# Rows turned by DMA instead of TensorE, and expert weights in a ring of three slots, in a mixture-of-experts stage on one core

## What is computed

```
logits = einsum('bld,ed->ble', layernorm(h) * rn_g + rn_b, router_w) + router_b
top_w, top_idx = top_k(logits, 2);  top_w = softmax(top_w)
for e in range(8):
    t = layernorm(h) * ln_g[e] + ln_b[e]
    t = gelu(t @ w1[e] + b1[e])          # 256 -> 1024, exact gelu
    t = t @ w2[e] + b2[e]                # 1024 -> 256
    out += combine[..., e] * t
x = x + gb * out
```

## Time and profile before

| | |
|---|---|
| three runs | 1261.82 us median, 1258.67 to 1263.27 |
| profiled execution | 1263.39 us |
| its span, first to last instruction | 1261.6 us |
| mean granted TensorE clock over the span | 0.909 |
| PE, DVE, ACT, POOL busy | 1123.1, 912.2, 554.1, 588.1 us |

### The profile page before, as it was taken

The page is one execution under the profiler, slowest core; times in us unless marked ns, Lnnn a source line. Parts: engine busy times, 40 slices in busy tenths (PEclk is TensorE's granted clock), DMA queues, the critical chain, the costliest instruction groups (busy, mean ns, idle before and its releaser), DMA issues.

```text
span 1261.6 us, 29766 instructions
## 1 busy us (share of the span) xinstructions
PE 1123.1 (89%) x8408; PEld 892.3 (71%) x8408; DVE 912.2 (72%) x2923; ACT 554.1 (44%) x1098; POOL 588.1 (47%) x487
## 2 busy tenths in 40 slices
PE   5789799889884329999999999999999999999996
PEld 1334454554443318998999999998999999998995
DVE  5577878877886426777777777777777777777775
ACT  1567565666563203433444444433434444433442
POOL 2111554554556572455554454445554444445553
PEclk8788878877796558999999999999999999999998
DMA  5346546556454265877444747457444444445743
GB/s 159 126 155 210 175 154 230 194 179 229 153 179 141 75 217 166 213 208 179 87 84 85 215 90 213 85 128 176 88 84 86 85 85 82 85 87 116 192 83 45
DMA packets 105765, 177.38 MB, mean 141 GB/s; under 512 B 23580, under 2 KB 76968, under 8 KB 99592
## 3 DMA queue, kind: packets, MB, share of 16 engines
q1 hardware_dynamic: 71560, 120.34, 30.7%
q0 software_dynamic: 34176, 56.72, 23.2%
HBM read 228.66 MB, written 63.69 MB: 232 GB/s over the span
## 4 chain that ended last, share of the span: by engine, by line
PE 71%; DVE 9%; issue 4%; POOL 3%; DMA 2%; another core or an unknown queue 1%; ACT 1%; DVEq 1%; POOLq 0%; SPq 0%; ACTq 0%
PE banks L1227 29%; PE banks L1215 29%; PE banks L1180 3%; PE banks L1204 3%; PE banks L1189 3%; DVE st L670 2%; POOL lists L461 2%; DMA lists<-nrm,slot 2%; PE banks L1101 2%; PE banks L1118 2%; DVE rowbuf L788 1%; DVE rowbuf L790 1%; DVE mv L675 1%; DVE resid L844 1%
## 5 line engine op out<-in xcount | busy, mean ns | idle before, releaser
L1215 PE MATMUL banks<-nh,wbuf 128*128 128x256 bf16 x2272 | 467.9, 274 | 9.8 <-ACT gf L641 8.3
L1227 PE MATMUL banks<-wbuf,resid 128*128 128x256 bf16 x3408 | 465.7, 273 | 0.0
L641 ACT ACTIVATE gf<-banks,b1t 128x256 f32<-128x256 f32 x568 | 269.3, 474 | 428.3 <-PE banks L1215 348.8
L497 POOL DMA_INDIRECT out<-rowbuf,ydst x142 | 232.0, 1634 | 353.2 <-DVE rowbuf L1008 279.5
L1227 PEld LDWEIGHTS banks<-wbuf,resid 128*128 128x128 bf16 x3408 | 334.1, 98 | 39.2
L1215 PE MATMUL banks<-nl,wbuf 128*128 128x256 bf16 x1136 | 311.1, 274 | 0.0
L1016 DVE CAST resid<-gf 128x256 bf16<-128x256 f32 x568 | 180.0, 317 | 178.6 <-ACT gf L641 110.9
L1018 DVE TENSOR_TENSOR resid<-gf,resid 128x256 bf16<-128x256 f32 x568 | 241.9, 426 | 19.5
L1215 PEld LDWEIGHTS banks<-nh,wbuf 128*128 128x128 bf16 x2272 | 223.2, 98 | 37.4 <-ACT gf L641 9.7
L461 POOL DMA_INDIRECT lists<-nrm,slot x128 | 138.4, 1081 | 142.2 <-DVE nrm L904 107.6
L488 POOL DMA_INDIRECT resid<-y_rows,ygb x142 | 145.3, 1023 | 54.9 <-issue 43.7
(11 more groups left out here) (184 smaller groups left out, 1101.5 us busy)
## 6 DMA issues: line engine op xcount, KB each, us to landing
wbuf<-wsplit SPq DMA_DIRECT2D x142, 1024.0 KB
rowbuf<-lists SPq DMA_DIRECT2D x71, 264.0 KB
wbuf<-in_L_ffn_w SPq DMA_DIRECT2D x16, 1024.0 KB, 6.7
wsplit<-wbuf SPq DMA_DIRECT2D x16, 1024.0 KB, 5.3
b2t<-in_L_ffn_b SPq DMA_DIRECT2D x71, 128.0 KB
resid<-in_L_attn_x SPq DMA_DIRECT2D x16, 512.0 KB, 7.4
out<-resid SPq DMA_DIRECT2D x16, 512.0 KB
csB<-mod_rows SPq DMA_DIRECT2D x16, 256.0 KB
```

Source lines behind the costliest of these rows:

```text
L497: g.indirect_dma_start(out_rows, bass.IndirectOffsetOnAxis(ap=ydst[:, r, h:h + 1], axis=0), yt[:, r, h, :], None, compute_op=ALU.add).then ...
L641: a.activation(gf[:, c % 2, :], MM[c % 2][:, 0:TOK], ACT.Gelu, bias=b1t[:, r, c:c + 1]).then_inc(gf_s, 1)
L1215: last = t.matmul(MM[c % 2][:, 0:TOK], w, m[:, r, k, :], start=n == 0, stop=n == 5)
L1227: last = t.matmul(ACC[r][h][:, 0:D], g[:, c, h * P:(h + 1) * P], w, start=c == 0 and n == 0, stop=c == NI - 1 and n == 2)
```

## The change

Rows: ACT's `head_rows` and DVE's `split_rows` now work on `xin` itself, in SBUF, for the tile two ahead, and write head and rest side by side into `xhl` (bf16, row-major). SP's new `flip` turns them with two transposing DMAs of 128 x 512 into `nhl`, from which `first` reads. PE's `turn` is gone. `rows_load` is issued a tile earlier, ahead of `flip`, and waits for `nl_s` and `yw_s` where it waited for `tr_s` and `yt_to`; `destinations` copies the token numbers into `ytok`, from which `targets` copies them.

Weights: `wring` has three slots, the first over the tail of the store that held `resid`. Expert e is in slot (e + 1) mod 3 and is loaded once: experts 0 and 1 ahead of all rows, expert e + 2 at the first tile of expert e (`weights_ahead`). The biases (`bias_load`) are loaded only when the flag of row 2 is set. `table` grows to 7 rows: slot of the tile's expert (row 3), whether to load ahead (4), which expert (5), into which slot (6). PE reads the slots of this tile and of the one before from row 3 into registers (`set_of`), and its weights' addresses come from them. The diff's core; it leaves out the declarations of semaphores, `ytok` and the copies of it:

```
+        store = sb("store", [P, NB * NC * D + 4 * NI * D])
+        wring = store[:, NB * NC * D - 2 * NI * D:].bitcast(bf16).rearrange("p (s n) -> p s n", s=3)
+        wbuf = wring[:, 1:3, :]
+        nhl = sb("nhl", [P, 2, 2 * NK, TOK], bf16)
+        xhl = sb("xhl", [P, 2, TH, 2 * D], bf16)
+        table = sb("table", [P, 7, TILES], i32); tab_c = sb("tab_c", [P, 2, TILES]); tab_m = sb("tab_m", [P, TILES])
...
             def rows_load(j, r):
                 row = nc.sync.value_load(table[0:1, 1, ds(j, 1)], min_val=0, max_val=DUMMY)
-                wait_past(sp, tr_s, j - 1)
-                wait_past(sp, yt_to, j - 1)
+                wait_past(sp, nl_s, j - 1)
+                wait_past(sp, yw_s, j - 1)
...
+            def entry(j, row, top):
+                return nc.sync.value_load(table[0:1, row, ds(j, 1)], min_val=0, max_val=top)
+            def weights_ahead(j, r):
+                e, new, s = entry(j, 5, E - 1), entry(j, 4, 1), entry(j, 6, 2)
+                sp.wait_ge(mm1_s, NI * j + 1)
+                sp.dma_start(wring[:, ds(s, 1), 0:4096], wsplit_d[ds(e, 1), :, 0:4096], cond=new).then_inc(got_w1[r], 16)
+                sp.wait_ge(mm2_s, NI * j + 1)
+                sp.dma_start(wring[:, ds(s, 1), 4096:8192], wsplit_d[ds(e, 1), :, 4096:8192], cond=new).then_inc(got_w2[r], 16)
+            def bias_load(j, r):
+                e, new = entry(j, 0, E - 1), entry(j, 2, 1)
+                wait_past(sp, gf_s, NI * (j - 1))
+                sp.dma_start(b1t[:, r, :], b1f_d[ds(e, 1)], cond=new).then_inc(got_b1[r], 16)
+                wait_past(sp, yb_s, j - 1)
+                sp.dma_start(b2t[:, r, :], b2_d[ds(e, 1), :].partition_broadcast(P), cond=new).then_inc(got_b2[r], 16)
+            def flip(j, r):
+                sp.wait_ge(nl_s, j + 1)
+                hold(sp, "sp")
                 wait_past(sp, mm1_s, NI * (j - 1))
+                hold(sp, "sp")
+                for h in range(TH):
+                    sp.dma_start_transpose(nhl[:, r, :, h * P:(h + 1) * P], xhl[:, r, h, :]).then_inc(got_nT[r], 16)
             def tile_loads(j, r):
-                rows_load(j, r)
-                e, new = which(j)
-                first_load(j, r, e, new)
-                second_load(j, r, e, new)
-            e, new = which(0)
-            first_load(0, 0, e, new)
+                if not isinstance(j, int) or j + 1 < TILES:
+                    rows_load(j + 1, 1 - r)
+                flip(j, r)
+                bias_load(j, r)
+                if not isinstance(j, int) or j + 1 < TILES:
+                    weights_ahead(j - 1, 1 - r)
+            for e in range(2):
+                sp.dma_start(wbuf[:, e, 0:4096], wsplit_d[e, :, 0:4096]).then_inc(got_p1[e], 16)
+                sp.dma_start(wbuf[:, e, 4096:8192], wsplit_d[e, :, 4096:8192]).then_inc(got_p2[e], 16)
             for r in range(2):
                 sp.wait_ge(scat[r], 16 * 2 * NC * NB // 2)
             sp.wait_ge(dummy_out, 16)
             rows_load(0, 0)
-            second_load(0, 0, e, new)
+            rows_load(1, 1)
+            bias_load(0, 0)
+            flip(0, 0)
+            sp.wait_ge(x2_out, 16 * NB)
...
-            def head_rows(j, r):
-                act.wait_ge(tr_s, j + 1)
-                wait_past(act, mm1_s, NI * (j - 1))
-                a.activation(nh[:, r, :, :].rearrange("p k n -> p (k n)"), TR[r][:, :], ACT.Copy).then_inc(nh_s, 1)
+            def head_rows(j, half, r):
+                act.wait_ge(got_xin[r], 16 * half + 16)
+                wait_past(act, got_nT[r], 16 * TH * half)
+                hold(act, "act")
+                a.activation(xhl[:, r, :, 0:D], xin[:, r, :, 0:D], ACT.Copy).then_inc(nh_s, 1)
...
             def split_rows(j, half, r):
                 dve.wait_ge(nh_s, j + 1)
+                v.tensor_tensor(xhl[:, r, :, D:2 * D], xin[:, r, :, 0:D],
+                                xhl[:, r, :, 0:D], ALU.subtract).then_inc(nl_s, 1)
...
-            def turn(j, half, r):
-                pe.wait_ge(got_xin[r], 16 * half + 16)
-                wait_past(pe, nl_s, j - 1)
-                for k in range(NK):
-                    for h in range(TH):
-                        last = t.transpose(TR[r][:, k * TOK + h * P:k * TOK + (h + 1) * P], xin[:, r, h, k * P:(k + 1) * P], ident[:, :])
-                last.then_inc(tr_s, 1)
+            def set_of(j):
+                return ds(nc.tensor.value_load(table[0:1, 3, ds(j, 1)], min_val=0, max_val=2), 1)
...
-                    head = wbuf[:, r, k * I + c * P:k * I + (c + 1) * P]
-                    rest = wbuf[:, r, 2048 + k * I + c * P:2048 + k * I + (c + 1) * P]
-                    for w, m in ((head, nh), (head, nl), (rest, nh)):
-                        last = t.matmul(MM[c % 2][:, 0:TOK], w, m[:, r, k, :], start=n == 0, stop=n == 5)
+                    head = wring[:, s, k * I + c * P:k * I + (c + 1) * P]
+                    rest = wring[:, s, 2048 + k * I + c * P:2048 + k * I + (c + 1) * P]
+                    for w, m in ((head, k), (head, NK + k), (rest, k)):
+                        last = t.matmul(MM[c % 2][:, 0:TOK], w, nhl[:, r, m, :], start=n == 0, stop=n == 5)
...
+            def tile(j, half, r, is_first):
+                now = set_of(j)
+                past = None if is_first else set_of(j - 1)
+                pe.wait_ge(got_nT[r], 16 * TH * half + 16 * TH)
...
+                    pe.wait_ge(got_w1[r], 16 * half)
...
+                    first(j, r, now, c)
...
+                        second(j, r, now, c - LAG)
                     elif not is_first:
+                        second(j - 1, 1 - r, past, NI - LAG + c)
-                    if c == 4 and not is_last:
-                        turn(j + 1, half + r, 1 - r)
```

More of the change, by code:

```diff
@@ L625, in _, with gelu @@
             pipeline(a, step)
[L628 to L634 removed]
+            def head_rows(j, half, r):
[3 more added lines that the diff above has]
+                a.activation(xhl[:, r, :, 0:D], xin[:, r, :, 0:D], ACT.Copy).then_inc(nh_s, 1)
+            def gelu(j, half, r):
                 act.wait_ge(got_b1[r], 16 * half + 16)
                 for c in range(NI):
[L637 to L638 removed]
+                    if c == 5 and not (isinstance(j, int) and j + 2 >= TILES):
+                        head_rows(j + 2, half + 1, r)
                     act.wait_ge(mm1_s, NI * j + c + 1)
@@ L641, in gelu @@
                     a.activation(gf[:, c % 2, :], MM[c % 2][:, 0:TOK], ACT.Gelu, bias=b1t[:, r, c:c + 1]).then_inc(gf_s, 1)
-            head_rows(0, 0)
+            for r in range(2):
+                head_rows(r, 0, r)
             for j in range(2):
                 gelu(j, 0, j)
-            with a.Fori(1, TILES // 2) as h:
+            with a.Fori(1, TILES // 2 - 1) as h:
                 for r in range(2):
                     gelu(2 * h + r, h, r)
-            for j in range(TILES // 2 * 2, TILES):
-                gelu(j, j // 2, j % 2, j == TILES - 1)
+            for j in range((TILES // 2 - 1) * 2, TILES):
+                gelu(j, j // 2, j % 2)
         @block.vector
@@ L1024, in tile @@
                         targets(j, half, r)
-                    if c == 5 and not last_tile:
-                        split_rows(j + 1, half + r, 1 - r)
+                    if c == 5 and not (isinstance(j, int) and j + 2 >= TILES):
+                        split_rows(j + 2, half + 1, r)
                     if c == 6 and not last_tile:
@@ L1030, in _ @@
             dve.wait_ge(x2_out, 16 * NB)
-            split_rows(0, 0, 0)
+            for r in range(2):
+                split_rows(r, 0, r)
             destinations(0, 0, 0)
@@ L1235, in tile @@
                 for c in range(NI):
-                    first(j, r, c)
+                    first(j, r, now, c)
                     if c >= LAG:
                         if c == LAG:
-                            pe.wait_ge(got_w2[r], 16 * half + 16)
+                            if isinstance(j, int) and j < 2:
+                                pe.wait_ge(got_p2[j], 16)
+                            else:
+                                pe.wait_ge(got_w2[r], 16 * half)
                             wait_past(pe, yb_s, j - 1)
-                        second(j, r, c - LAG)
+                            hold(pe, "pe")
+                        second(j, r, now, c - LAG)
@@ L1242, in tile @@
                     elif not is_first:
-                        second(j - 1, 1 - r, NI - LAG + c)
-                    if c == 4 and not is_last:
-                        turn(j + 1, half + r, 1 - r)
-            turn(0, 0, 0)
+                        second(j - 1, 1 - r, past, NI - LAG + c)
+            pe.wait_ge(tab_s, 1)
+            hold(pe, "pe")
             for j in range(3):
-                tile(j, j // 2, j % 2, j == 0, False)
+                tile(j, j // 2, j % 2, j == 0)
             with t.Fori(1, (TILES - 1) // 2 - 1) as h:
-                tile(2 * h + 1, h, 1, False, False)
-                tile(2 * h + 2, h + 1, 0, False, False)
```

(7 more changed lines are left out.)

61 lines of the change are left out of this document (29 added, 32 removed).

## The result

The changed kernel took **1286.18 us** (median of 4 runs, 1280.62 to 1292.49) against 1261.97: a ratio of 1.0195, interval 1.0172 to 1.0219. It is slower, where the prediction had 1251, faster. Run again beside the experiments it took 1283.41 (1280.02 to 1287.15), ratio 1.0158, 1.0125 to 1.0191. The profiled execution is the fastest of the first four, 1280.62 us, with a span of 1278.8, 17.2 more than before.

What follows compares the result with a forecast made beforehand. The prediction took PE, busy throughout the main MoE stretch, as the bound. From 1263.4 us it subtracted 17 for the removed turns net of edge bubbles and added 5 for a later start: 1251, range 1230 to 1290.

Steps and rivals of the forecast that it cites:

- What bounds the kernel: MoE stage: PE is busy throughout, period 10.91 us per tile, chunks 1.31 us; only array time or gaps in it count.
- The 30.8 us of the turns: PE in the MoE: 70 turns inside tiles removed at 0.44 us each; the period could be 10.48 us.
- Rows through DMA: SP's queue and flips: transposes take 4 us, hidden, 8 at the slow end; SP needs 6.7 of 10.5 us per tile.
- The mean over two tiles: PE's tile edges: series work of 2.05 to 2.4 us against a 1.85 us lead leaves a bubble, taken as 0.2 us.
- the gain of 17: MoE tiles on PE: period 10.68 us, 0.24 us saved on each of 70; bounds 30.8 and 8 us.
- the 1.1 preferred: PE's tile edge: two table reads in series, priced at 1.1 to 1.46 us.
- the rows behind the weights: SP's queue in the tiles: rows land about 1 us into a tile, head_rows wants them 6.5 us in; no cost.
- the fourth rival: Tiles: transposes or SP come late and PE waits; 1345, or 1270 if only behind six later experts' weights; chance 0.07.
- The start: Start of the MoE stage: rows land behind 4 MB of weights, first matmul likely at 472; −4 to +8 us, taken as +5.
- The first: Rival, stage start: weights, slow transposes and ACT's gaps cost 12 to 15 us against 17; 1260, no change; chance 0.10.
- The second: Rival, PE's tile edges: table reads cost more than on SP, 0.87 us each, mean bubble 0.6; 1280, milder 1263; chance 0.15.
- The third: Rival, PE's sequencer becomes the bound, addresses worked out anew per matmul; 1480 to 1550, or 1317 with nine per chunk; chance 0.13.

## Why the prediction was wrong

- **What bounds the kernel** held: PE, with chunks of 1.31 us as before, and a period of 10.48 us once nothing interrupts it (no register, no reads). The 30.8 us of the turns were real.
- **Rows through DMA** held as far as the transposes go. Each of a flip's two transposes holds SP 1.28 us (median, below) and not 0.33, so SP's tile is nearer 9 than 6.7 us, still inside 10.5; a flip's last packet was written 4.8 us after its first issue in the median and 8.6 at the latest, where I took 4, with 8 as the slow bound; PE's only wait for a flip in the table of its waits is the stage's first, here from 470 to 480 us behind the row of the issue.

```profile
L391 SPq DMA_TRANSPOSE nhl<-xhl x142: 697/1282/3124, 473.1 to 1245.1; - x142
```

```profile
PE banks L1245 <- DMA nhl<-xhl: 37.0, 1, 37.0
```

- **The step that failed: "The mean over two tiles is 0.1 to 0.33; I take 0.2. Period 10.68, gain 0.24 × 70 = 17 us."** The mechanism, a chain in series at the edge against the sequencer's lead, is the one the runs show, down to the two lengths of edge. It was mis-sized. The gaps are 0.80 and 0.19 (0.8 × 33 + 0.19 × 34 = 33 us), a mean of 0.5, and that is more than the 0.44 of the turn: the gain of 17 is a loss of 2 to 4. The reads take 0.75 and 0.64, 1.4 together, above the 1.1 preferred but inside its 1.46. What went past the bounds was the rest: waits, hold and address take 0.6 for 0.5, and above all the lead at the branch is 1.6 and not 1.85. The lead was taken over from the kernel before without asking whether the change touches it. The addresses went into the sequencer's sum, which held, and one of them into the chain; they did not go into the lead, though they take over the waits for the gelu. Their number was right, 6 per chunk of 568, and so nearly was their price: 46 ns, 0.124 us apart, for the 0.1 I had. Their rows (ns min/median/max):

```profile
L1245 PEldq FUSED_REGOPS  x2272: 46/46/65, 474.9 to 1262.7; - x190
...
L1257 PEldq FUSED_REGOPS  x1136: 46/46/60, 479.6 to 1266.1; - x190
```

  From 806 us on the lead is 1.85 in every kernel here with constant addresses, those with the reads among them, and 1.34 to 1.72 in the changed kernel and with one read.
- **The second term that was short: the rows behind the weights, at nothing.** The prediction says what would happen if they were late (ACT's gelu queued behind head_rows) and has "if only behind the 2 MB of each of six later experts, 6 × 3 us" as the mild end of the fourth rival, with too small a chance. It was 10 us, and came as written, with one thing more: a chunk that waits for its gelu also leaves less lead for the next edge.
- **The start** was right: +5 forecast, +3.6 measured in this trace, the rows in by 467.7 (when `head_rows` starts) for 464 to 470, the first matmul at 475.04 for 472, chunk 3 at 479.75, 4.7 behind it, for 4.4. The start varies by several us from trace to trace, so that it came this close is in part luck.
- The terms as measured close for the profiled execution: 1263.4 − 31 + 33 to 35 + 10 + 3.6 = 1279 to 1281, against 1280.6. What puts the median of its four runs 5.6 above that, no run shows.
- **The rivals.** The first did not come: chunk 3 started before 484. The second had the time (1280), its sign (a gap near 0.8, though only at every second edge) and the wrong cause: a read's load is 298 ns at that edge and 302 in the median on PE, not 600, and the read 0.64 to 0.75, not 0.87. The floor of about 600 ns that the Trainium skill's "DMA: Bandwidth & Descriptors" states in Latency and other measured facts holds for the whole read at most, by these rows, and not for the load. The third did not come: addresses are used again within a chunk, and PE was full with them when one read was left. The 62 ns per MATMUL that the Trainium skill's "TensorE: Matmul & The Clock Gate" gives in Step-by-step: what each phase is for, where no hardware decoder does it, did not show: an estimate by it, 12 × 0.062 beside six address operations of 0.124, is 1.49 us a chunk, and with register addresses twelve matmuls still start within 1.31 us. The fourth came in its mild form, at the loads and not at every tile.

## What to carry to other kernels

Work on a sequencer is not priced by its sum against the array's time but where it stands in series: read off how far the sequencer is ahead of the array at that place, in the code as it will be (here register addresses took the lead from 1.85 to 1.6 us, because a wait that had been on a weight load stood on an address operation, where the sequencer waits with it), and keep branch, table reads and waits together below it, or spread the reads into the middle of the tile. Here the same two reads a tile cost 12 us or nothing, by their place alone. And a large transfer is put on a queue by what is issued next behind it: with 2 MB ahead of the small rows, ACT waited 19.3 us for rows, with the 2 MB behind the flip 0.2; the 7.5 us that then remained were PE's wait for weights that it did not need yet.

## What was not expected of the hardware

A transposing DMA of 128 x 512 bf16 held SP for 1.28 us in the median, and up to 3.1, where a plain one of 264 KB held it for 0.33. And a table read on TensorE runs beside the matmuls already issued: some 140 of them in mid-tile left no gap. A wait on an address operation is another matter: it holds the sequencer, and with it the lead.
